# A graph network's edge layer: nine tiles of a block picked and nine fetched, compares made by whole tiles, all messages in two fp16 terms, and a second pair of banks in the turn between two layers

## The reference

```python
h = jnp.maximum(_layernorm(x, axis=-1), 0.0)
# layers one and two: two times
#   agg = segment_sum(h[src], dst) / cnt ;  h = relu(agg @ W_l + h @ W_r + b)
x = x + _L0_gnn_ref(h, edge_index, ...)
h = jnp.maximum(_layernorm(x, axis=-1), 0.0)
# layer three
h_edge = jnp.concatenate([h[src], h[dst]], axis=-1)
m_ij = jax.nn.relu(h_edge @ W_interact + b_interact)
m_i = jax.ops.segment_sum(m_ij, src, num_segments=6250) / sqrt(16)
x = x + (h + jax.nn.relu((h + m_i) @ W_update + b_update))
```

## Time and profile before

| what | value |
|---|---|
| median of 3 runs | 1626.95 us (1626.29 to 1627.2) |
| the profiled execution | 1626.57 us, its span 1624.8 us |
| PE busy | 1361.5 us, 84% |
| DVE busy | 1323.4 us, 81% |
| POOL busy | 960.9 us, 59% |
| ACT busy | 870.3 us, 54% |

### The profile page before, as it was taken

One profiled execution on the slowest core, in us unless ns is written; L12 is line 12 of the kernel. 1 busy time (PEld: TensorE's weight loads), 2 busy tenths in 40 slices (PEclk: granted clock), 3 DMA queues, 4 the chain that ended last, 5 costly groups with the idle time before them and its releaser, 6 DMA issues.

```text
span 1624.8 us, 38769 instructions
## 1 busy us (share of the span) xinstructions
PE 1361.5 (84%) x14368; PEld 1157.3 (71%) x14368; DVE 1323.4 (81%) x4011; ACT 870.3 (54%) x1635; POOL 960.9 (59%) x982
## 2 busy tenths in 40 slices
PE   1523797999999988999998599898898988999887
PEld 1312576777777756777776588888898888988887
DVE  7968797999999546777666588888988889888887
ACT  1634676787778630100012556566666666666664
POOL 5363705787770016777720377777777777777773
PEclk9855898999999999999998789999999999999999
DMA  3003734646655048999972334444443444444442
GB/s 115 1 1 109 257 142 144 248 177 210 226 172 207 25 124 278 307 314 299 303 243 87 77 108 124 110 129 116 121 118 106 124 119 119 108 109 120 120 115 58
DMA packets 123382, 243.23 MB, mean 150 GB/s; under 512 B 20984, under 2 KB 75401, under 8 KB 123194
## 3 DMA queue, kind: packets, MB, share of 16 engines
q1 hardware_dynamic: 95179, 186.10, 34.3%
q0 software_dynamic: 26432, 54.06, 13.3%
q10 hardware_dynamic: 1584, 0.59, 0.1%
HBM read 170.73 MB, written 73.14 MB: 150 GB/s over the span
## 4 chain that ended last, share of the span: by engine, by line
DVE 41%; PE 35%; issue 10%; ACT 8%; DMA 3%; SPq 1%; DVEq 1%; POOL 0%; ACTq 0%; POOLq 0%
PE ps L1245 12%; DVE room L2162 8%; PE ps L1229 5%; DVE hot L1794 4%; PE ps L1452 4%; ACT lnw L1108 3%; DVE ps L2192 3%; PE ps L1218 3%; ACT slab L1130 2%; DVE slab L2162 2%; DVE hot L2154 2%; PE ps L1285 2%; DVE hot L1789 2%; DVE keys L1920 2%; DVE keys L1919 2%
## 5 line engine op out<-in xcount | busy, mean ns | idle before, releaser
L999 ACT ACTIVATE slab<-ps 128x980 f16<-128x980 f32 x256 | 321.3, 1277 | 120.3 <-PE ps L1218 104.6
L910 POOL DMA_INDIRECT cells<-b_rows,work x270 | 264.6, 980 | 98.2 <-issue 69.2
L1452 PE MATMUL ps<-slab,room 125*128 125x128 f16 x3538 | 238.4, 221 | 35.0 <-DVE room L2162 34.4
L1229 PE MATMUL ps<-slab,room 128*128 128x320 f16 x1568 | 252.2, 301 | 0.1
L1452 PEld LDWEIGHTS ps<-slab,room 125*128 125x128 f16 x3538 | 209.2, 99 | 46.2 <-DVE room L2162 45.8
L1245 PE MATMUL ps<-slab,room 128*128 128x320 f16 x1568 | 226.7, 300 | 0.0
L1443 PE MATMUL ps<-inv,hot 125*128 125x128 f16 x1800 | 216.4, 220 | 2.3 <-DVE hot L2154 2.3
L1218 PE MATMUL ps<-hot 128*128 128x245 bf16 x1024 | 161.2, 282 | 50.1 <-DVE hot L1794 38.9
L874 POOL DMA_INDIRECT hot<-t_rows,pairs x160 | 165.7, 1036 | 55.7 <-issue 48.2
L2162 DVE TENSOR_SCALAR room<-keys,up_c 125x256 f16<-125x256 f16 (+3 forms) x908 | 196.8, 297 | 0.0
L1245 PEld LDWEIGHTS ps<-slab,room 128*128 128x128 f16 x1568 | 153.3, 98 | 59.2 <-issue 2.6
(11 more groups left out here) (363 smaller groups left out, 2539.0 us busy)
## 6 DMA issues: line engine op xcount, KB each, us to landing
slabs_d<-slab SPq DMA_DIRECT2D x14, 3920.0 KB, 14.1
slab<-slabs_d SPq DMA_DIRECT2D x98, 560.0 KB, 5.3
hot<-lane_d SPq DMA_DIRECT2D x50, 576.0 KB
keys<-up_d SPq DMA_DIRECT2D x50, 160.0 KB
inv<-inv_row SPq DMA_DIRECT2D x32, 160.0 KB, 7.6
keys<-down_d SPq DMA_DIRECT2D x50, 96.0 KB
cells<-b_rows,work POOLq DMA_INDIRECT x270
t_rows<-room SPq DMA_DIRECT2D x1, 3200.0 KB, 13.7
```

What stands on the lines that cost most here:

```text
L910: p.indirect_dma_start(rows_g[gi % RS][:, j, :], None, b_rows, bass.IndirectOffsetOnAxis(ap=node_t[:, t:t + 1], axis=0)).then_inc(e_gath[g ...
L999: a.activation(slab[par][:, :, u * UB * BW:(u + 1) * UB * BW].rearrange("p h (k d) -> p k h d", k=UB), psum_unit(u).rearrange("p k (h d) - ...
L1229: last = t.matmul(ps[:, 4 + s % 2, 0:SC], table[:, h, term, :], slab[s % 2][:, h, :], start=k == 0, stop=k == HI * HALVES - 1)
L1452: last = t.matmul(to, end_hot[g // 3][0:BN, u:u + P], bt[0:BN, bt_at(tile, w), k, :], start=False, stop=w == w1 - 1 and k == HALVES - 1)
```

## The change

Layer three has another table of groups: tile 14 becomes a picked tile, so nine are picked and nine fetched, and the picked tiles are dealt to other groups. The one-hots of a picked tile are made by one TENSOR_TENSOR over its whole window, with the tile's row repeated over the units and the units' numbers (now fp16, kept in pairs) repeated over the columns; numbers and targets are shifted by 512 (`MIDDLE`). The rows of the targets of odd blocks move to another place in SBUF (`end_row[1]`). All six groups have messages of two fp16 terms. TensorE's `source_sum` goes four groups behind instead of three, VectorE's `low_term` goes one group behind, ahead of `prepare`, and `keep_sum`, `whole_sum`, `biased` and `residual` get other places. In the turn, `own_product` of layer two writes the banks 4 and 5 for even chunks and 6 and 7 for odd ones (`own_bank`).

```diff
-    GROUPS = (((0, 1), (5,)), ((2, 3), (6,)), ((4,), (7, 8)), ((15,), (9, 10)), ((16,), (11, 12)), ((17,), (13, 14)))
-    UP, DOWN = (0, 1, 2, 3, 4), (15, 16, 17)
-    SPLIT_GROUPS = (0, 2, 5)
+    GROUPS = (((0, 3), (5,)), ((1, 2), (6,)), ((4,), (7, 8)), ((14, 17), (9,)), ((15,), (10, 11)), ((16,), (12, 13)))
+    UP, DOWN = (0, 1, 2, 3, 4), (14, 15, 16, 17)
...
-        up_c = sb("up_c", [P, UPW])
-        down_c = sb("down_c", [P, UPW])
+        up_c = sb("up_c", [P, UPW, 2], f16)
+        down_c = sb("down_c", [P, UPW, 2], f16)
+        lane_c = sb("lane_c", [P, 1])
...
+        def own_bank(L, c):
+            return 4 if L and c % 2 == 0 else 6
+
...
-        end_row = last_N[:, :].bitcast(f16)[:, 0:2 * len(ENDS) * P].rearrange("p (s n) -> p s n", s=2)
+        o = 2 * NB * D + HOT_UNITS[0] * P
+        end_row = [last_N[:, :].bitcast(f16)[:, 0:len(ENDS) * P], room_b.bitcast(f16)[:, o:o + len(ENDS) * P]]
...
-                to = msg_split[gi % 3][:, :, 0, :] if gi % GB in SPLIT_GROUPS else msg[gi % 3]
-                a.activation(to, ps[:, gi % 4, 0:GW].rearrange("p (j f) -> p j f", j=GT), ACT.Relu).then_inc(e_msg, 1)
+                a.activation(msg[gi % 3][:, :, 0, :], ps[:, gi % 4, 0:GW].rearrange("p (j f) -> p j f", j=GT), ACT.Relu
+                             ).then_inc(e_msg, 1)
...
-                if c:
-                    pe.wait_ge(S["own_ok"], c)
+                if c > L:
+                    pe.wait_ge(S["own_ok"], c - L)
...
-                    last = t.matmul(ps[:, 6 + h, 0:HALF], wr[L][:, :], of[:, h * HALF:(h + 1) * HALF],
+                    last = t.matmul(ps[:, own_bank(L, c) + h, 0:HALF], wr[L][:, :], of[:, h * HALF:(h + 1) * HALF],
...
+                    if q == 0:
+                        pe.wait_ge(PS_[1]["own_ok"], NC - 1)
...
-                    pe.wait_ge(e_msg, gi - 3)
-                    if (gi - 4) % GB in SPLIT_GROUPS:
-                        pe.wait_ge(e_low, splits(gi - 4))
+                    pe.wait_ge(e_low, gi - 3)
...
-                    last = t.matmul(ps[0:BE, 4 + b % 2, 0:2 * D if split else D], src_hot[gi % 6][:, j, :], of,
+                    last = t.matmul(ps[0:BE, 4 + b % 2, 0:2 * D], src_hot[gi % 6][:, j, :],
+                                    msg[gi % 3][:, j, :, :].rearrange("p k f -> p (k f)"),
...
-                if gi > 2:
-                    source_sum(gi - 3)
+                if gi > 3:
+                    source_sum(gi - 4)
...
-                for w, t0, n, at in batch:
-                    row = end_row[0:BN, b % 2, t0 * P:(t0 + n) * P]
-                    last = v.tensor_scalar(end_hot[h][0:BN, at * P:(at + n) * P], row, numbers[0:BN, w:w + 1], None,
-                                           ALU.is_equal)
-                if batch:
-                    last.then_inc(e_endhot, 1)
+                for tile, w0, w1, at in SIDES[b, h][0][g % 3]:
+                    both = [BN, w1 - w0, P // 2, 2]
+                    row = end_row[b % 2][0:BN, ENDS.index(tile) * P:(ENDS.index(tile) + 1) * P]
+                    last = v.tensor_tensor(
+                        out=end_hot[h][0:BN, at * P:(at + w1 - w0) * P].rearrange("p (w n e) -> p w n e", n=P // 2, e=2),
+                        in0=row.rearrange("p (n e) -> p n e", e=2).unsqueeze(1).to_broadcast(both),
+                        in1=numbers[0:BN, w0:w1, :].unsqueeze(2).to_broadcast(both), op=ALU.is_equal)
+                last.then_inc(e_endhot, 1)
...
                 add_rows(gi)
+                if gi:
+                    low_term(gi - 1)
                 if gi + AHEAD < NGR:
                     prepare(gi + AHEAD)
-                low_term(gi)
-                if gi + AHEAD < NGR:
                     source_hot(gi + AHEAD)
                 if g == 2 and b + 1 < NB:
                     split_lo(b + 1)
-                if g == AHEAD and b:
+                if g == 2 and b > 1:
+                    keep_sum(b - 2)
+                if g == 4 and b:
                     whole_sum(b - 1)
-                if g == 3 and b > 1:
-                    keep_sum(b - 2)
-                if g == 0 and b - 3 in LAST_BLOCK:
-                    biased(LAST_BLOCK.index(b - 3))
-                if g == 2 and b - 3 in LAST_BLOCK:
+                if g == GB - 1 and b - 2 in LAST_BLOCK:
+                    biased(LAST_BLOCK.index(b - 2))
+                if g == 1 and b - 3 in LAST_BLOCK:
                     residual(LAST_BLOCK.index(b - 3))
```

More of the change, by code:

```diff
@@ L104, in gnn_kernel @@
     EDGES = 5
-    assert N == NB * BN and NB == CT * NC and sorted(sum(TILES, ())) == list(range(TB)) and KU <= P and NB <= HH * HL <= 64 and QT % TH == 0 and 64 * PADS == FH * (P - KP)
+    assert N == NB * BN and NB == CT * NC and sorted(sum(TILES, ())) == list(range(TB)) and KU <= P and UPW * BN - MIDDLE <= 2048 and NB <= HH * HL <= 64 and QT % TH == 0 and 64 * PADS == FH * (P - KP)
     assert NG == 2 * HG and NTILE % KT == 0 and HG <= P and NT == CT * NC and NC == 10
@@ L156, in side_plan @@
     def side_plan(b, h):
-        tiles = UP if h == 0 else DOWN
-        at, made, unit = 0, [], {}
+        at, made = 0, []
         for picked, _ in GROUPS[3 * h:3 * h + 3]:
             made.append([])
[L161 to L171, removed]
+            for tile in picked:
+                w0, w1 = window(b, tile)
+                made[-1].append((tile, w0, w1, at))
+                at += w1 - w0
+        return made, {tile: first - w0 for batch in made for tile, w0, _, first in batch}, at
     SIDES = {(b, h): side_plan(b, h) for b in range(NB) for h in range(2)}
     HOT_UNITS = [max(SIDES[b, h][2] for b in range(NB)) for h in range(2)]
[L175 to L179, removed]
     def bt_at(end, w):
@@ L530, in chunk @@
             return hT[:, c * CW:(c + 1) * CW]
-        def splits(gi):
-            return sum(g % GB in SPLIT_GROUPS for g in range(gi + 1))
         def hots(gi):
@@ L1446, in edge_sum @@
                         if j == 0:
-                            pe.wait_ge(e_endhot, HOTS[gi])
+                            pe.wait_ge(e_endhot, gi + 1)
                         w0, w1 = window(b, tile)
                         for w in range(w0, w1):
-                            u = unit[w, tile] * P
+                            u = (unit[tile] + w) * P
                             for k in range(HALVES):
@@ L2080, in _ @@
                 dve.wait_ge(S["own"], c + 1)
-                v.tensor_scalar(chunk(c).rearrange("p (h n) -> p h n", h=2), ps[:, 6:8, 0:HALF], bc[1][:, 0:1], None,
-                                ALU.add).then_inc(S["own_ok"], 1)
+                at = own_bank(1, c)
+                v.tensor_scalar(chunk(c).rearrange("p (h n) -> p h n", h=2), ps[:, at:at + 2, 0:HALF], bc[1][:, 0:1],
+                                None, ALU.add).then_inc(S["own_ok"], 1)
             second_layer()
@@ L2153, in prepare @@
                     lanes_of = row_lane[0:BN, b % 2, :]
-                    v.tensor_scalar(lanes_of, lanes_of, up_c[0:BN, 0:1], None, ALU.is_equal).then_inc(e_rowhot, 1)
+                    v.tensor_scalar(lanes_of, lanes_of, lane_c[0:BN, 0:1], None, ALU.is_equal).then_inc(e_rowhot, 1)
                 h = g // 3
@@ L2195, in low_term @@
             def low_term(gi):
-                if gi % GB not in SPLIT_GROUPS:
-                    return
                 dve.wait_ge(e_msg, gi + 1)
```

36 lines of the change are left out of this document (17 added, 19 removed).

## The result

The changed kernel takes 1585.28 us (median of 4 runs, 1582.7 to 1588.01), the kernel before 1626.62 beside it: a ratio of 0.9755, with a 95% interval of 0.9737 to 0.9774. That is 41 us less, where 80.6 were forecast. The profiled execution took 1582.7 us, its span 1580.9.

What follows compares the result with a forecast made beforehand. VectorE's ordered list was taken to set layer three's pace. A block falling from 13.51 to 12.0 us saves 75.5 us, the turn 5.5: 1626.6 - 75.5 - 5.5 = 1546 us, with some 8 in 10 from 1524 to 1588.

Steps and rivals of the forecast that it cites:

- The step that failed is GpSimd's: Layer three's fetches: nine a block instead of ten, taken at 1.30 us each with issue, 11.7 us a block.
- the bound of 1.39 from layer one: Upper price of a layer-three fetch, from 14 fetches in layer one beside two-input compares: 12.5 us a block.
- rival A: GpSimd becomes layer three's bound: 1.39 us a fetch plus 0.2 of landing waits, 12.7 us a block, 1581 us; chance 0.14.
- The lower bound of that step, 1.24 us: Lower price of a fetch with its issue, as in layer three before the change: 11.2 us a block.
- The rule that the prediction quoted: Two-SBUF-input tensor_tensor contends only with GpSimd instructions reading SBUF; by it, layer-three fetches cost at most 1.24 us each.
- Compares: Picked-tile compares on VectorE, layer three: 0.08 us fixed plus 0.065 per 128 columns, 238 us for 296, balance -58 us.
- rival B: Layer three's new compares do not run two columns a cycle: 0.13 us a unit, 1741 us; chance 0.06.
- VectorE's work: VectorE's list in layer three, small compares traded for low terms: +6 us in all, 11.9 us a block.
- The wait for ScalarE: VectorE's 64.3 us wait in layer three for ScalarE's message-bank eviction, ahead of the low term, costed at nothing after the change.
- The update: TensorE's output updates in layer three: nine waits of 2.65 us for the kept sum go, plus 9 us of slow clock.
- TensorE: TensorE's list in layer three: +47 us matmuls, -64.5 us source sums, -26 us with the clock, 11.8 us a block.
- The turn: Between layers one and two, two bank pairs save 0.72 us in each of eight rounds, 5.5 us taken.

Runs made afterwards that it cites:

- e4: The changed kernel with each paired compare cut in two instructions of half the columns, one behind the other: 1609.04 us.
- e10: The kernel of e2 with the order of before: low term in the group's own turn, source sum three groups behind: 1565.91 us.
- e2: The changed kernel with eight fetches a block instead of nine, one left out from the tenth group on: 1524.02 us.
- e1: The kernel before with only layer two's own products taking two pairs of banks in turn, layer three unchanged: 1618.13 us.
- e7: The changed kernel with the low term made for one of a group's three tiles only: 1558.51 us.

## Why the prediction was wrong

The step that failed is GpSimd's: "VectorE would be in such an instruction for (238 + 100 x 0.26)/50 = 5.3 us of a block, less than half the time, so I take 1.30, 11.7 us." A fetch measured 1.44 us with its issue, above even the bound of 1.39 from layer one, and nine of them bound the block: 13.07 us once GpSimd's lead is used up, 12.77 in the mean. That is rival A, which had 1581 us; it was held less likely than the forecast for the same wrong reason. That its 12.7 us a block is so near the mean is in part luck: it took 1.39 a fetch, less than they cost, and added 0.2 for landings. The step treated the price as a share of time, so that half the compares stretch a fetch half as much. The runs show a hold instead: in the changed kernel a fetch that starts under a row addition takes 0.94 us every time (42, by the count under e4), and one that starts under a paired compare 1.30 in the mean (170), however much of the fetch lies beside it. What counts is how often a fetch starts under a compare, for how long that compare still runs, and whether another follows at once. Before, with TENSOR_SCALAR compares of some 0.2 us each, the same meeting cost 0.02 us in the mean (202 fetches, 0.96 us); only the lane compare held fetches for long (35 of 36, 1.33 us in the mean).

The lower bound of that step, 1.24 us, was too low as well, so that 1.30 left next to nothing for the new compares. It comes from one of the three groups of fetches, and some of their issues are counted there as waits for VectorE. The page of the kernel before has the other two:

```profile
L910 POOL DMA_INDIRECT cell_lo<-b_rows,work x115 | 115.7, 1006 | 41.2 <-issue 26.8
L910 POOL DMA_INDIRECT cell_hi<-b_rows,work x115 | 116.0, 1009 | 38.8 <-issue 28.3
```

All 492 fetches together took 488.33 us, 0.99 each, and with 0.30 of issue a fetch cost 1.30 us before the change. GpSimd was thus at it for some 638 of the 662 us; its 488 us of busy time leave the issues out.

The rule that the prediction quoted from the Trainium skill (SBUF — State Buffer, section "Who interferes with whom") does not come out here as the prediction applied it. It says that an instruction with two SBUF inputs contends with a GpSimd instruction that reads SBUF, and not with one that only writes. The prediction counted a fetch as one that only writes, and so got 1.24 us at most; the traces fit the rule if a fetch reads SBUF early on (its row numbers lie there), though no run here shows what it reads. Under instructions with one input in PSUM (the row addition, `hrow<-ps,bias`, 6 of 6, and the low term, 70 of 100) it takes 0.94 us, and the other 30 under low terms all met the lane compare, as the last section shows; under those with two inputs in SBUF it is held, an fp32 one too (`slab<-hrow,slab`, 5 of 6, up to 1.63).

The other steps, in their order. *Compares*: the forms of 640 and 1152 columns take 0.485 and 0.751 us, 0.0665 us per 128 columns (0.065 was taken), so rival B was rightly priced out. *VectorE's work*: 11.9 us a block forecast, 571.25/49 = 11.66 busy. *The wait for ScalarE*: gone, as forecast; e10 shows what the order is worth where VectorE bounds, 0.8 us a block. *The update*: 100 matmuls, and TensorE waits for the kept sum once, 0.4 us, not 24.5; nine of the ten updates take 1.33 us, where six took 2.0 to 2.5. *TensorE*: 11.8 us forecast; e2 is busy 559.09/49 = 11.41. With one fetch less these fit in 11.65 us a block (e2), under the forecast of 12.0, so VectorE's, ScalarE's and TensorE's steps were right or a little cautious. *The turn*: 5.5 us forecast, 7.4 measured in e1 (5 to 11 by its interval).

## What to carry to other kernels

When a change swaps many short VectorE instructions for a few long ones with two SBUF inputs, look at what GpSimd issues meanwhile, and count its issues with its busy time: an indirect fetch that starts under one waits for its end (165 of 170 here), so price the fetch by the length of the instruction it meets, not by a share of time. Put an instruction that reads PSUM between two such compares; that order alone gave 24 us here. And when three engines' lists are forecast within 0.2 us of each other, the least known price of the three, and not the largest sum, decides.

## What the runs showed of the hardware that was not expected

A fetch takes 0.94 us, or it ends 0.82 us behind the end of the paired compare that was running when it started (210 of 210 in e10). Who comes first decides: over the eleven kernels with paired compares, 540 fetches met one that began 0.02 to 0.2 us behind their own start and did not follow another compare, and none was held by it. Where another compare follows without a gap, the held fetch is sometimes passed over and waits for that one too: 33 of 59 in the changed kernel, 63 of 142 with halves, none of 46 in e10. The 33 all started 0.11 to 0.14 us before the second compare began, but in e7 15 that started so were not passed over; what decides stays open. The lane compare, a TENSOR_SCALAR of 2304 columns, holds at a second point as well. In the changed kernel it began 0.17 to 0.26 us behind the start of 30 fetches, and all 30 ended 0.12 us behind its end. One is the fetch of 1005.83, which starts before it, and ends 0.11 us after it (1006.83) with 1.11 us in all:

```profile
1005.83 1.11 POOL L901 DMA_INDIRECT cell_hi<-b_rows,work  x1 [0.30 <-issue]
1006.01 0.82 DVE L2143 TENSOR_SCALAR hot<-hot,lane_c 125x2304 f16<-125x2304 f16 x1
```

Here too the first one wins: where it began 0.48 to 0.53 us behind the fetch's start (three cases), the fetch took 0.94 us and the lane compare 1.00 to 1.04 instead of 0.81. No paired compare holds at that point, as the 540 show: the fetch of 1010.55 above, too, ran under one to its end at 0.94 us. The Trainium skill (same page and section) says that a tensor_scalar in a two-port mode shuts GpSimd out altogether, and a tensor_tensor only from reading; the two rows above agree with that if the lane compare ran in such a mode and the second point is a write, neither of which a run here shows.
